# Keys of two heads rotated after a product that lays them out turned, value tiles projected for four heads at once

## What is computed

```
lat = layer_norm(layer_norm(x))          ctx = layer_norm(context)
q = (lat @ Wq)                           k, v = split(ctx @ Wkv)
k = [k1*cos - k2*sin, k2*cos + k1*sin]   # halves of 32 of each head; cos, sin by context row
a = softmax(clip(q k^T / 8, -11, 11))
x = x + tanh(g) * ((a v) @ Wo + bo)
```

## Time and profile before

| | |
|---|---|
| median of 3 runs | 2723.12 us (2722.44 to 2727.2) |
| the profiled execution | 2726.36 us, span 2724.6 us, granted clock 0.96 |
| busy: TensorE, VectorE, GpSimd, ScalarE | 89%, 78%, 73%, 43% of the span |
| attention, first to last projection | 60 us to about 2060 us |
| batch 0, batch 1, batches 2 to 6 | 236, 244, 254 to 256 us each |

### The profile page before, as it was taken

How to read it: one execution, slowest core, us unless ns; L and a number is a source line. 1 busy time by engine, 2 the same in 40 slices (tenths; PEclk the granted TensorE clock), 3 DMA queues, 4 the chain that set the end, 5 groups by cost and what they waited for, 6 DMA issues and landing times. The chain is left out here.

```text
span 2724.6 us, 47912 instructions
## 1 busy us (share of the span) xinstructions
PE 2419.1 (89%) x13494; PEld 1471.9 (54%) x13494; DVE 2125.0 (78%) x4785; ACT 1163.4 (43%) x2652; POOL 1989.4 (73%) x2550
## 2 busy tenths in 40 slices
PE   2999999999989998999999899989996986998991
PEld 1555555555555555555555555545553655987780
DVE  4877788887888787878778787888787666688884
ACT  2444444444344444443444344344442332676660
POOL 2777677689868886988698789868885731067776
PEclk9999999999989998999899999999997997999995
DMA  8334334111111211111121111111111516799994
GB/s 302 136 123 147 109 109 148 47 45 49 49 46 48 69 47 45 49 51 54 40 67 50 48 45 49 49 46 50 68 47 53 198 38 239 238 309 318 328 324 148
DMA packets 157368, 301.61 MB, mean 111 GB/s; under 512 B 20066, under 2 KB 95778, under 8 KB 156834
## 3 DMA queue, kind: packets, MB, share of 16 engines
q1 hardware_dynamic: 128994, 230.95, 25.0%
q0 software_dynamic: 24576, 67.14, 7.5%
q10 hardware_dynamic: 3520, 0.27, 0.1%
HBM read 170.37 MB, written 127.93 MB: 109 GB/s over the span
## 5 line engine op out<-in xcount | busy, mean ns | idle before, releaser
L925 ACT ACTIVATE e<-scores 128x1024 f32<-128x1024 f32 x520 | 533.9, 1027 | 920.0 <-PE scores L807 897.3
L1020 POOL TENSOR_SCALAR e<-e 128x1024 f32<-128x1024 f32 x520 | 613.7, 1180 | 50.4 <-ACT e L925 6.9
L1200 DVE TENSOR_TENSOR e_sum<-e_sum,e 128x1024 f32<-128x1024 f32 x391 | 582.1, 1489 | 5.7 <-POOL e L1020 5.5
L847 PE MATMUL ps_o<-e,v 128*64 128x512 f32 x2088 | 567.5, 622 | 0.4 <-POOL e L1020 0.4
L807 PE MATMUL scores<-q_t,k_t 64*128 64x512 f32 x3120 | 503.8, 427 | 28.9 <-DVE affine L1143 13.9
L819 PE MATMUL ps_kv<-w,ctx_t 128*128 128x256 f32 x3072 | 507.7, 302 | 11.9 <-DVE ctx_t L1150 8.5
L819 PEld LDWEIGHTS ps_kv<-w,ctx_t 128*128 128x128 f32 x3072 | 401.4, 191 | 202.0 <-issue 173.5
L807 PEld LDWEIGHTS scores<-q_t,k_t 64*128 64x128 f32 x3120 | 257.5, 185 | 391.3 <-issue 251.5
L1728 POOL DMA_INDIRECT room<-results_in_blocks,index x256 | 247.0, 965 | 210.4 <-DMA results_in_blocks<-room 130.5
L1010 POOL TENSOR_TENSOR k_rot<-rope_c,rope_s 128x64 f32<-128x64 f32 x513 | 323.2, 630 | 68.4 <-PE ps_kt L837 23.0
L1014 POOL TENSOR_TENSOR k_rot<-rope_c,rope_s 128x64 f32<-128x64 f32 x513 | 203.6, 397 | 195.3 <-ACT e L925 193.0
(11 more groups left out here) (287 smaller groups left out, 3553.3 us busy)
## 6 DMA issues: line engine op xcount, KB each, us to landing
w<-w_pairs SPq DMA_DIRECT2D x65, 768.0 KB, 4.5
rows_in_blocks<-room SPq DMA_DIRECT2D x16, 2560.0 KB, 11.3
x_nat<-rows_in_blocks SPq DMA_DIRECT2D x160, 256.0 KB
results_in_blocks<-room SPq DMA_DIRECT2D x80, 512.0 KB
wo<-in_L_xattn_Wo SPq DMA_DIRECT2D x66, 128.0 KB, 4.5
x_nat<-in_ctx SPq DMA_DIRECT2D x64, 128.0 KB, 4.3
down_all<-in_L_ffn_down_w SPq DMA_DIRECT2D x16, 512.0 KB, 8.6
w_pairs<-w_split SPq DMA_DIRECT2D x8, 768.0 KB, 7.1
```

The costliest lines, as they stand in the source:

```text
L847: mm = pe.matmul(ps_o[hh * DH:(hh + 1) * DH, :], v[:, buf, tile, hh * DH:(hh + 1) * DH], e[:, tile % 4, hh * N:(hh + 1) * N], start=(tile ...
L925: act.activation(e[:, c % 4], scores[:, c % 2], ACT.Exp, scale=SCALE).then_inc(s_exp, 1)
L1020: pool.tensor_scalar(e[:, c % 4], e[:, c % 4], EXP_HI, EXP_LO, ALU.min, ALU.max).then_inc(s_clip, 1)
L1200: dve.tensor_tensor(total, e[:, 0] if c == 2 else total, e[:, tile % 4], ALU.add).then_inc(s_sum, 1)
```

## The change

The two halves of the keys-and-values product are taken apart.

**Keys.** The weights are now stationary and the context moves: twice a pair, at steps 0 and 4, six products of 512 columns (L928 of the changed kernel) give 512 rows of keys already turned, channels on the partitions, in `ps_k`. The transposes are gone. ScalarE copies the four blocks of 32 channels crosswise into `k_sw` (four instructions of 32x512), VectorE multiplies `ps_k` by cos and `k_sw` by sin (tables now turned and repeated over the channels, with the sign in sin; 128x512 each, at steps 1 and 5), GpSimd adds them (`k_c`, one instruction of 128x512 at steps 2 and 6), ScalarE writes the rounded part (steps 3 and 7) and VectorE the remainder (steps 4 and 7; `k_c` less the rounded part).

**Queries** are projected at step 2, also into `ps_k`, which so holds first keys, then queries, then keys in a pair: L940 waits for `s_cos` of the first half, and the keys at step 4 wait for `s_qlo`, the remainder of the queries, which VectorE now takes at step 3.

**Values** of two pairs (four heads, a *double*) come out of one product of 256 columns. In the first pair of a batch there are eight such tiles, one a step; in pairs 1 to 6 four each, at steps 3, 5, 6, 7 or at 1, 3, 5, 7; in pair 7 none. In batch 0 each even pair has eight and each odd pair none. In total there are 4 x 8 tiles a batch.

The boundary turns the context first and the latents last. GpSimd normalises the output in two halves (before the clip of step 3 and after that of step 4), and its scatters stand at steps 0, 1, 4, 5 and 7 of pairs 1 to 6, with one in pair 0 and one in pair 7. Slots and gates of the router go to DRAM after each batch instead of being copied on the core, and come back after the attention; the turned tables are made in `setup`. The diff, cut to the steps of the attention:

```
 # TensorE, step
+                tile = value_tile(p, m, c) if project else None
+                if tile is not None:
...
+                            mm = pe.matmul(ps_v[:, 0:2 * P], ctx_t[:, a, cc, tile * P:(tile + 1) * P], wv[:, bb, cc],
...
-                            mm = pe.matmul(ps_kv[:, 0:2 * P], ctx_t[:, a, cc, c * P:(c + 1) * P],
-                                           w[:, jj, bb, cc, 1:3].rearrange("p t m -> p (t m)"),
...
-                    pe.transpose(ps_kt[:, 0:P], k_rot[:, c % 2].rearrange("p h d -> p (h d)"), pers.ident[:]
-                                 ).then_inc(s_kt, 1)
+                if project and c in (0, 4):
+                    half = c // 4
...
+                        pe.wait_ge(s_qlo, 2 + g)
+                    pe.wait_ge(s_cos, 1 + g * 2 + half)
...
+                            mm = pe.matmul(ps_k[:], wqk[:, jj, bb, cc, 1], ctx_t[:, a, cc, half * N:(half + 1) * N],
...
+                if project and c == 2:
...
+                            mm = pe.matmul(ps_k[:], wqk[:, jj, bb, cc, 0], lat_t[:, a, cc, :],
 # ScalarE, step
-                    act.activation(v[:, jj, c], ps_kv[:, P:2 * P], ACT.Copy).then_inc(s_v, 1)
+                    act.activation(v[:, tile, both], ps_v[:, 0:2 * P].rearrange("p (t n) -> p t n", t=2), ACT.Copy
...
+                    for q in range(4):
+                        to, of = slice(q * 32, (q + 1) * 32), slice((q ^ 1) * 32, (q ^ 1) * 32 + 32)
+                        st = act.activation(k_sw[to], ps_k[of], ACT.Copy)
+                    st.then_inc(s_swapped, 1)
...
+                    act.activation(k_t[:, jj, 0, half * N:(half + 1) * N], k_c[:], ACT.Copy).then_inc(s_khi, 1)
 # GpSimd, step
-                    pool.tensor_tensor(k_rot[:, buf, :, 0:DH // 2], rope_c[:, buf, :, 0:DH // 2],
-                                       rope_s[:, buf, :, DH // 2:DH], ALU.subtract)
...
-                    pool.tensor_tensor(k_rot[:, buf, :, DH // 2:DH], rope_c[:, buf, :, DH // 2:DH],
-                                       rope_s[:, buf, :, 0:DH // 2], ALU.add).then_inc(s_rot, 1)
+                if project and c in (2, 6):
+                    half = c // 4
+                    pool.wait_ge(s_sin, g * 2 + half + 1)
+                    pool.tensor_tensor(k_c[:], k_c[:], k_sw[:], ALU.add).then_inc(s_turned, 1)
 # VectorE, step
-                    for table, dst in ((pers.cos, rope_c), (pers.sin, rope_s)):
...
-                    dve.tensor_tensor(k_t[:, buf, 1, tile], ps_kt[:, 0:P], f32(k_t[:, buf, 0, tile]), ALU.subtract
...
+                    dve.tensor_tensor(k_c[:], ps_k[:], rope.cos[:, tokens], ALU.mult).then_inc(s_cos, 1)
+                    dve.tensor_tensor(k_sw[:], k_sw[:], rope.sin[:, tokens], ALU.mult).then_inc(s_sin, 1)
...
+                    dve.tensor_tensor(k_t[:, jj, 1, tokens], k_c[:], f32(k_t[:, jj, 0, tokens]), ALU.subtract
```

399 lines of the change are left out of this document (242 added, 157 removed).

## The result

The changed kernel takes 2638.01 us (median, 2635.58 to 2643.14), beside 2722.78 for the kernel before: ratio 0.9688, 95% interval 0.967 to 0.9707. It is faster by 85 us, where I had forecast 161; my range was 2522 to 2612.

What follows compares the result with a forecast made beforehand. The prediction took TensorE to be the bound. 134 us of its work, 26 and 3 of idle time, less 2 of setup, made 161: 2565 from the profiled 2726.4, stated as 2562 us; range 2522 to 2612.

Steps and rivals of the forecast that it cites:

- TensorE's own work: Keys and values in each attention pair: 8.16 us would become 6.06, saving 2.10 a pair, 134 us over 64 pairs.
- My fallback of 1.55: Key product on TensorE priced at the row's duration, 1.55 us, instead of its pitch: the gain would be 114 us.
- VectorE's term: VectorE in each attention pair: 6.7 us removed, 4.3 added, a net loss of 2.4, counted as only 1 to 2.
- Idle time: TensorE's idle time in a middle batch: 13.7 us instead of 18.1, 26 us over six batches, 3 in batches 0 and 1.
- The waits for GpSimd: TensorE's waits in even pairs, 2 to 3 us each, should fall to about 1.
- pair 7's end: VectorE bounds pair 7 at about 26 us; TensorE would idle 6.5 us there instead of 5.1.
- The waits stay: Rival, chance 0.22: VectorE and GpSimd keep TensorE waiting in the attention; 106 to 134 us won, 2590 to 2617.
- no difference: Case with chance 0.03: both the waits and the 512-column price go wrong together.
- The slower rival: Rival, chance 0.04: queries' remainder late in each pair's `ps_k` chain; 4 us later gives all back, 5 makes about 2805.
- The shared port: Rival, chance 0.05: VectorE and GpSimd contend for SBUF ports, VectorE has 5.7 us more in each pair: 2680.
- Setup: Eight more splits on ScalarE and on VectorE before the attention would cost 2 us.
- the loads after the attention: Two more loads ahead of the experts' weights would cost 0, or at most 5 us if they came after.

Runs made afterwards that it cites:

- e4: The changed kernel with VectorE's product of the swapped key halves and the sines left out, keys not fully turned: 93.5 us below the kernel before.
- e6: The changed kernel with value tiles moved beside key and query products, and at steps 4 and 6 both behind e*v: 46.7 us below the kernel before.
- e1: The changed kernel with an unread 128-column transpose behind 512-column key and query products, 147 in all: 70.1 us below the kernel before.
- the control: The changed kernel run again unedited, as the foot of comparisons: 80.8 us below the kernel before.
- e14: The changed kernel with only the value tiles moved to the steps of key and query products: 31.3 us below the kernel before.
- e16: The changed kernel with a later boundary wait, filler products and the router's `second_of_group` moved from step 1 to 3 of pair 5: 103.2 us below the kernel before.
- e5: The changed kernel unedited, run as the control: 80.8 us below the kernel before.

## Why the prediction was wrong

**TensorE's own work** failed, in the step that said "so its price is nearly sure". The form was indeed the queries' form to the letter, but 1.39 was the pitch between two products of the same tiling. By the pitches, the work removed is 9.55 (8.16 and the 1.39 of the queries), and what replaces it 2 x 1.59 + 1.60 + 4 x 0.90 = 8.38: 1.17 us a pair or 75 us, where I had 134. In eleven pairs tiles stand right ahead of key and query products (0.82 and 1.48 there), which makes it 81. Measured are 93 of busy time, 96 at full clock. Of the other 15, small delays inside the busy time of the kernel before are 12: 6 in e\*v, 6 in keys, values and transposes, added up from start to start. My fallback of 1.55, "the duration of that row", came nearest, and I had set it aside. I charged each product alone and never asked what a removed transpose had done for its neighbours: it cost some 0.10, not 0.20. Of the 76 us that the forecast was off, this term is 41 (134 less 93), and idle time, below, 34 (29 less forecast, 5 more measured).

**VectorE's term** failed as a sum and as a sign. Forecast 1 to 2 us a pair less; measured 1 more (213.04 - 205.19 = 7.9 a batch). The new instructions of 128x512 have means of 0.89 (L1282) and 0.93 (L1287), for 0.74 assumed, and the 24 small ones were spaced at some 0.2 in the trace, 4.8 us a pair instead of 6.7. By these figures the new ones take only 0.2 a pair more. Of VectorE's 43 us more in the attention, 23 are the norms' L90 (means of 0.41 and 0.64 us before, 0.70 and 0.94 after) and 12 the sums of the exponentials, neither of which I had priced; why they take longer was not tried. But e4 says that the sum mattered little.

**Idle time.** The waits for GpSimd went, as forecast, in part by luck: I had read them as waits for the rotated keys alone, and the larger part was for the normalised output. Pair 4 has 0.14 us of idle time left (I had 0.7), pair 5 1.7 (1.3), the boundary's last wait 1.8 (1.9), pair 7's end 6.6 (6.5). What I had missed in pair 7 is 3.1 us at step 4 on top of that end: I named the place and priced it at "about 1 us". VectorE runs without a break there, so the router work ahead of the remainder makes it late. Pair 2 has 2.7 us for 1.5, of which 2.1 is the wait of the router's transposes for `x`, which I had not named, and pair 6 1.4 for 0.8. With small gains elsewhere that makes 17.4 instead of 13.7 a batch. Batch 1 adds 5 us that I had not looked at: 14.7 against 9.1.

**The rivals.** "The waits stay" was nearest, at 106 to 134 for a gain of 85: it had the sum of the waits about right, though not their places (pair 4's went), with the wrong price of the work. I gave it 0.22, and let no case combine a wrong price with waits that stay, except "no difference". The slower rival's chain through `ps_k` exists, in pairs 5 and 7, and not in each pair. The shared port did not become the bound: the sums of exponentials have a mean of 1.50 us (1.49 in the earlier trace rows). Its price of 2680 also fails by its own figures: 250 us a batch takes 30 for all eight pairs, and with 27.4 in the five without router work it would be 238 and some 2580. And in the earlier trace rows clip and sum overlap for 0.72 us, of which the sum loses 0.58. Setup cost 0.2 us for the 2 forecast, and the loads after the attention nothing, as forecast.

## What to carry to other kernels

Price a matrix product by a pitch with the same neighbours as it will have, not by its own form: a change of tiling costs on either side. After removing work from an engine that waits at fixed places, walk those places one by one, since here the average load of the engine waited for said little (e4). And count a wait of TensorE's with the clock behind it; filling an unavoidable wait with products that nobody reads is cheap, but look for where the stretch at half clock turns up next.

## What the runs showed of the hardware

- A product over 128\*128 costs 0.10 us more behind one of another tiling, and 0.10 more ahead of one: 1.39, 1.49 and 1.59 us for the same six instructions of 512 columns (e6, e1, the control), with 64\*128 ahead and 128\*64 behind, and 0.82 and 0.91 for 256 columns that begin behind scores.
- The clock reacts to how the waits lie, not to their sum. The kernel before has 118.8 us of idle time and 89 at half clock, e4 104.1 and 136, e14 149.1 and 205. In the twenty traces' attention stages there are 429 half-clock stretches, and all but one begin during a wait of TensorE's of over 0.9 us or within 3 us behind it. The reverse doesn't hold: of the waits of 1.9 to 2.2 us 119 of 191 had such a stretch. In e16 one began 0.2 us behind a wait of 2.08 us (ended at 1189.5) and one within a wait of 3.07 (ended at 1214.9); in the control e5 waits of 2.09 (ended at 1082.7) and 3.07 (ended at 1219.3) had none. A stretch of 3.4 us cost a pair about 1.6 us (29.2 to 30.8 in columns 2 and 5). The Trainium skill, page "TensorE: Matmul & The Clock Gate", section "Loop structure matters more than you think", has a long wait between products make the engine run cold; the boundary agrees (a wait of 6.58 us, with half clock from 1.5 us before its end over the transposes), and shorter waits do so too here. What decides for a given wait stays open.
- Outside the attention, all kernels took 841 to 849 us in some runs and 699 to 701 in others, on the same chip; the DMA rate in the experts' stage was then 220 to 250 GB/s instead of 310 to 330. Why was not tried.
